# A routed convolution and windowed attention on one core: the three silus of an image issued in two parts

## The reference

```python
x = x + _L0_conv_ref(_gn(x), ...)      # routed convolution
x = x + _L1_conv_ref(_gn(x), ...)      # attention in 8x8 windows, and a 7x7 depthwise convolution of v

# _L0_conv_ref: a shared 1x1 group convolution and two of eight 3x3 experts per image
shared = silu(group_norm(conv(x, shared_w)))
en = group_norm(conv(x, expert))                 # for each of the two chosen experts
return shared + (silu(en) * rw).sum(axis=1)

# _L1_conv_ref: per window of 64 tokens, 8 heads of 16
scores = q @ k.T / sqrt(16) + bias
o = softmax(scores) @ v
out = proj(o + depthwise(v)) + proj_b
```

## Time and profile before

| | |
|---|---|
| time, median of 3 runs | 931.99 us (929.11 to 934.04) |
| time of the profiled execution | 934.59 us |
| its span, first to last instruction | 932.9 us |
| mean granted PE clock | 0.879 of full |
| PE busy | 743.6 us, 80% |
| DVE busy | 578.1 us, 62% |
| ACT busy | 457.7 us, 49% |
| POOL busy | 197.0 us, 21% |

### The profile page before, as it was taken

The page is one execution under the profiler, slowest core; times in us unless marked ns, Lnnn a source line. Parts: engine busy times, 40 slices in busy tenths (PEclk is TensorE's granted clock), DMA queues, the critical chain, the costliest instruction groups (busy, mean ns, idle before and its releaser), DMA issues.

```text
span 932.9 us, 18414 instructions
## 1 busy us (share of the span) xinstructions
PE 743.6 (80%) x6926; PEld 422.7 (45%) x6926; DVE 578.1 (62%) x1136; ACT 457.7 (49%) x746; POOL 197.0 (21%) x289
## 2 busy tenths in 40 slices
PE   6143768888888989888989887979797989978785
PEld 5121334454545554545454545454545456534321
DVE  4724456675767666767676757575757587632296
ACT  1204546555555564646464646464646465344422
POOL 3122123131213140403130313131313020000044
PEclk9976969797979797979888988888988989999999
DMA  9224444545464545455554545454546254586435
GB/s 353 106 71 116 139 113 146 145 128 156 144 178 136 163 148 150 150 153 165 142 170 128 173 136 173 123 173 120 177 132 177 67 176 132 161 276 217 156 157 203
DMA packets 84046, 145.29 MB, mean 156 GB/s; under 512 B 24179, under 2 KB 48886, under 8 KB 83958
## 3 DMA queue, kind: packets, MB, share of 16 engines
q1 hardware_dynamic: 58102, 100.89, 34.8%
q0 software_dynamic: 21248, 25.36, 10.9%
q10 hardware_dynamic: 4608, 17.86, 5.2%
HBM read 84.21 MB, written 51.41 MB: 145 GB/s over the span
## 4 chain that ended last, share of the span: by engine, by line
PE 41%; DMA 19%; DVE 16%; ACT 8%; issue 7%; SPq 6%; POOL 1%; POOLq 1%; ACTq 0%; DVEq 0%
PE g L1061 11%; DMA sk_d<-khl 10%; PE g L1057 5%; PE g L1079 4%; PE t L1127 4%; DMA stack<-sk_d 3%; SPq L298 3%; ACT xw L540 3%; PE s L1116 3%; PE pv L1142 3%; DMA vt<-x 3%; PE t L1241 2%; PE s L1112 2%; SPq L292 2%; PE s L1241 2%
## 5 line engine op out<-in xcount | busy, mean ns | idle before, releaser
L806 DVE BATCH_NORM_STATS2 st<-y 128x6 f32<-128x512 f32 x96 | 66.6, 694 | 147.6 <-ACT y L522 147.6
L522 ACT ACTIVATE y<-g 128x512 f32<-128x512 f32 x96 | 57.2, 596 | 167.0 <-PE g L1061 87.0
L1061 PE MATMUL g<-xsh,wsel 96*128 96x512 f32 x256 | 127.8, 627 | 14.0 <-DMA xsh<-xs 10.5
L595 ACT ACTIVATE pt<-t 128x512 f32<-128x512 f32 x128 | 76.2, 597 | 118.8 <-PE t L1127 112.2
L870 DVE TENSOR_REDUCE mx<-s 128x8 f32<-128x512 f32 x128 | 87.8, 686 | 69.6 <-PE s L1116 69.6
L1127 PE MATMUL t<-ident,less 128*128 128x128 f32 x512 | 97.6, 321 | 3.7 <-DVE less L874 3.7
L1142 PE MATMUL pv<-vp,pt 128*64 128x34 f32 x2048 | 95.2, 242 | 5.0 <-ACT pt L595 4.8
L1112 PE MATMUL s<-bias,ident 128*128 128x512 f16 x128 | 56.7, 443 | 52.9 <-DMA stack<-sk_d 52.8
L1142 PEld LDWEIGHTS pv<-vp,pt 128*64 128x64 f32 x2048 | 80.1, 154 | 31.4 <-issue 25.0
L874 DVE TENSOR_TENSOR less<-s,mx 128x512 f32<-128x512 f32 x128 | 88.5, 692 | 4.4
L1079 PE MATMUL g<-xw,w 128*128 128x512 f32 x128 | 66.7, 640 | 15.4 <-ACT y L522 11.7
(11 more groups left out here) (159 smaller groups left out, 1158.5 us busy)
## 6 DMA issues: line engine op xcount, KB each, us to landing
xsh<-xs POOLq DMA_DIRECT2D x64, 210.0 KB, 5.4
stack<-sq_d SPq DMA_DIRECT2D x96, 128.0 KB, 3.1
stack<-sk_d SPq DMA_DIRECT2D x192, 64.0 KB, 2.8
xs<-xn ACTq DMA_DIRECT2D x16, 578.0 KB, 2.9
vt<-x SPq DMA_DIRECT2D x4, 2048.0 KB, 17.7
xin<-x POOLq DMA_DIRECT2D x16, 512.0 KB, 5.8
acc_d<-xr SPq DMA_DIRECT2D x16, 512.0 KB, 5.5
sq_d<-qhl SPq DMA_DIRECT2D x16, 512.0 KB, 7.7
```

The lines of the kernel that those rows point to most:

```text
L522: act.activation(y[:, k, h * HALF:(h + 1) * HALF], g[h][:, :], ACT.Identity).then_inc(g_free[h], 1)
L595: act.activation(pt[:, p % 2].rearrange("p i w n -> p (i w n)"), tbk[p % 2][:, :], ACT.Exp).then_inc(sem["exp_done"], 1)
L806: last = v.bn_stats(st[:, 2 * k + h, :], y[:, k, h * HALF:(h + 1) * HALF])
L1061: last = mm(g[h][:, :], wsel[:, k - 1, C * dy:C * dy + C], xsh[:, k - 1, dy + 16 * h:dy + 16 * h + 16, 0:W], start=(dy == 0), stop=(dy == 1))
```

## The change

The three silus of image b+2 stood together in front of the exponential of pair 6 (the seventh). Now only `silu(b + 2, 0)` stands there; the other two stand in front of the exponential of pair 7 (the eighth), and so behind the exponential of pair 6 and behind `vt_out(b + 1)`. ACT's order over these pairs was silu 0, silu 1, silu 2, exponential 6, vt_out, exponential 7; it is silu 0, exponential 6, vt_out, silu 1, silu 2, exponential 7. Nothing else is changed; the table loads on ACT are put in by the compiler, in front of an operation that needs another table than the one that is loaded.

```diff
             def step(b, has1, has2, has3):
                 for p in range(PAIRS):
                     if has2 and p == 6:
-                        for k in range(3):
-                            silu(b + 2, k)
+                        silu(b + 2, 0)
+                    if has2 and p == 7:
+                        silu(b + 2, 1)
+                        silu(b + 2, 2)
                     exponential(b, p)
```

## The result

| | before | changed |
|---|---|---|
| time, median | 931.79 us (4 runs) | 942.77 us (4 runs, 942.38 to 951.63) |
| profiled execution | 934.59 us | 942.40 us |
| its span | 932.9 us | 940.7 us |
| busy PE / DVE / ACT | 743.6 / 578.1 / 457.7 us | 745.3 / 577.5 / 494.4 us |

The changed kernel is slower: ratio 1.0142, interval 1.0077 to 1.0207, 11.0 us between the medians and 13.2 between the means. Times in this document are medians over all executions; a ratio is of means, over the executions within 1.5% of the fastest of their kernel, which leaves out one of the kernel before (940.27 us) and two of one experiment (947.66, its profiled one, and 1183.37). The forecast was 944.5 us, between 936.5 and 955, slower by 12.3 us.

The account below looks back on a forecast made before the run. The path was taken to run from stacked rows landing through DVE's maxima and additions to PE's `average`. Ten steps' 13.98 us less 1.66 gave 12.3 us over, 946.9 or 944.3, forecast 944.5, range 936.5 to 955.

Parts of the forecast that it names:

- The loads: On ACT, in each of 14 steps with silus: four table loads in place of two, a switch costing 1.3 us.
- Rival 4: Each load in front of silu 1 costs double in its new place, silu 1 at S+12.60: 46.4 us, 978; chance 0.03.
- Silu 1 gates xr and `average`: Silu 1 done at S+10.04 delays L841 by 1.40 us, putting `average` at S+14.71; forecast 944.5 us, chance 0.78.
- S: Start of the table load before an image's silus on ACT; zero point of the step's times, 432.85 in the example.
- Exponential 7 has cover: Late exponential 7 falls into PE's idle time; its matmuls end at S+14.17, 0.54 us ahead of `average`.
- only the late silu 1 counts: Of both delays before `average`, silu 1's 1.40 us reaches it; exponential 7, 2.70 us later, mostly fits PE's idle time.
- Rival 3 in its small form: Matmuls behind exponential 7 pass up to 1 us per image beyond the margin: 14 more, 958; most of rival's 0.09.
- No delay is absorbed, and the clock gives nothing: After `average` no wait swallows delay; PE's clock effect taken as 0, within bounds of −10.3 and +5.1 us.
- Rival 2: PE regains full clock early in every image, net +2.0, 934; or loads are hidden, 932 or so; together 0.10.
- Rival 3's large form: PE and DVE pass on all 2.70 us of late exponential 7, 37.8 us, 970; both forms together 0.09.
- The sum: Over the kernel: 13.98 us of delay in ten steps, less 1.66 us in the last, makes 12.3 us.
- rows 6: Profile rows before: 14 stretches from S to L841, 128.34 us in sum; four late ones counted as delay 0.

Follow-up runs that it names:

- the second measurement: The changed kernel run again with no edit, against the kernel before: 944.65 us against 932.29, ratio 1.0145.

## Why the prediction was right

- *The loads.* 29 and 29, 1.283 us each, as forecast. A switch costs what its row shows: from the start of a load to the next ACT instruction it is 1.29 to 1.30 us in all four places of all steps, and the load in front of silu 1 starts as soon as the copies end. Rival 4 falls. By the Trainium skill (ScalarE: Activation LUTs, What ACT_TABLE_LOAD costs) another 1380 ns for draining belong to each switch; no row of after or of the experiments shows them, and the measurement decides.
- *Silu 1 gates xr and `average`.* S+10.04 was worked out, L841 (now L843) started at S+10.08 to 10.10 in thirteen steps, and `average` at S+14.76 where 14.71 was forecast. Moving the silus further back cost 38.5 us, with PE free of exponentials in thirteen of fourteen steps: shown.
- *Exponential 7 has cover, 0.54 us of it.* PE idled 0.54 us in front of `average` behind late value matmuls. But "only the late silu 1 counts" was true of the order alone. With silu 1 on time the same exponential costs 5.4 us, and with `average` out of the way about 16. To bring silu 1 forward alone thus saved only half. To bring the exponential forward alone should save nothing, since `average` waits for DVE; no run shows that by itself. Rival 3 in its small form counted on the matmuls reaching past `average`; they ended 0.54 us in front of it.
- *No delay is absorbed, and the clock gives nothing.* From `average` to the next S: 413.98 after, 413.99 before. Rival 2 falls; its other form, loads that are hidden, falls with silu 1 done at S+10.05. Rival 3's large form (37.8 us) falls with it.
- *The sum.* 12.3 us forecast, 11.47 in the profiled pair, 12.2 in the profile of the second measurement, 11.0 and 12.4 between the medians, 13.2 and 13.5 between the means. The small excess over the first pair has its place in rows 6: I took the three late steps 10.59, 10.72 and 10.28 as given, and in the changed kernel they were 10.08 to 10.09, as all but the first. In the first two of the three the score matmuls of the stacked rows began sooner behind S (7.50 and 7.35 us, for 8.04 and 8.15 before). That is −1.3 us; the 0.05 us by which each of the others was longer gives about +0.6 back. It is a draw of the execution and no effect of the edit that I can show: in the second measurement two steps were late again (10.38 and 10.70 us). From S to L843 the stretches came to 141.4 us, and to 142.1 in the second measurement, where about 142 was forecast.

## What to carry to other kernels

An engine that is busy half of the time can still set the time in one place: work the new order out from the start of the stretch, and compare each end with the instruction that needs it. Splitting a run of one activation function around another one cost two more table loads per split here, 2.6 us of ACT; what reaches the time depends on what waits behind them, between 5 and 39 us for four orders with the same loads. When two chains end within half a microsecond of each other, find the idle engine behind both: here PE stood waiting for a result that nobody needed for some time yet, and moving that matmul back by half a convolution gained 14 to 16 us, while every other order of the silus tried here lost.

## What the hardware showed that I had not expected

DVE and GpSimd hold each other up. L841, with two inputs in SBUF, takes 1.28 us alone and 1.87 us beside GpSimd's copy and subtraction; the subtraction takes 2.12 us alone and 2.98 us when L841 runs as it starts. In the rows of before, L841 took 2.95 us beside a subtraction that had started 0.26 us sooner and L841 ended 1.09 us behind the end of that subtraction. With the second branch early it ended 1.07 us behind the end of the copy. Had it stood still until GpSimd was done, both would be its 1.28 us; they come 0.2 us short of that. So this nearly fits what the Trainium skill says (SBUF — State Buffer, SBUF: two separate sides), that the port pair shared by these two engines is held for a whole instruction and the other one blocks; the experiments did not measure the lock by itself.
